# Attention on one core: the row maximum over 1024 keys as one reduction over two PSUM banks, with two score banks instead of four

## The reference

```
attn = einsum('bhcnd,bhcmd->bhcnm', q, k) * scale      # 1024 x 1024 for each head and chunk
attn = softmax(attn, axis=-1)                          # needs the maximum over the 1024 keys
o = einsum('bhcnm,bhcmd->bhcnd', attn, v)
out = o @ Wp.T + bp
```

## Time and profile before

| | us |
|---|---|
| median of 3 runs | 13767.46 (13765.76 to 13772.49) |
| the profiled execution, span | 13760.1 |
| outside the span, median less span | 7.4 |
| PE busy | 12819.6 (93%) |
| DVE busy | 9806.3 (71%) |
| ACT busy | 7890.2 (57%) |
| attention, first to last maximum reduction | 4550.0 to 12863.5 |

### The profile page before, as it was taken

One profiled execution on the slowest core, in us unless ns is written; L12 is line 12 of the kernel. 1 busy time (PEld: TensorE's weight loads), 2 busy tenths in 40 slices (PEclk: granted clock), 3 DMA queues, 4 the chain that ended last, 5 costly groups with the idle time before them and its releaser, 6 DMA issues. The chain is left out here.

```text
span 13760.1 us, 258672 instructions
## 1 busy us (share of the span) xinstructions
PE 12819.6 (93%) x76348; PEld 5285.8 (38%) x76348; DVE 9806.3 (71%) x18034; ACT 7890.2 (57%) x14774; POOL 2684.0 (20%) x2692
## 2 busy tenths in 40 slices
PE   6999999999993799999999999999999999999899
PEld 3545544544552233333333333333333333333233
DVE  7888888888886676777777777777777777677411
ACT  4666666666663365666665666666666666566511
POOL 3445444444441000000000000000000000000144
PEclk9999999999996799999999999999999999999999
DMA  2110110101104222222222232222222222222254
GB/s 73 21 21 15 21 20 16 21 15 21 21 15 134 67 61 67 65 62 63 67 65 63 61 71 63 60 68 66 61 62 66 67 63 61 66 63 64 62 127 105
DMA packets 853449, 773.62 MB, mean 56 GB/s; under 512 B 587076, under 2 KB 621348, under 8 KB 840740
## 3 DMA queue, kind: packets, MB, share of 16 engines
q1 hardware_dynamic: 850468, 747.29, 24.0%
q10 hardware_dynamic: 1536, 8.39, 0.3%
HBM read 510.50 MB, written 244.96 MB: 55 GB/s over the span
## 5 line engine op out<-in xcount | busy, mean ns | idle before, releaser
L1495 DVE TENSOR_REDUCE a_big<-a_mp 128x1 f32<-128x512 f32 x8192 | 5225.0, 685 | 2325.0 <-PE a_mp L1328 2060.3
L1414 ACT ACTIVATE a_ex<-a_sc 128x512 f32<-128x512 f32 x8192 | 4450.3, 599 | 2366.1 <-PE a_sc L1316 2121.6
L1328 PE MATMUL a_mp<-a_ks,a_qs 108*128 108x512 bf16 x8192 | 3188.5, 389 | 188.5 <-DVE a_big L1495 86.1
L1316 PE MATMUL a_sc<-a_qs,a_ks 111*128 111x512 bf16 x8192 | 3157.0, 387 | 125.3 <-issue 80.6
L849 DVE TENSOR_TENSOR r_prod<-r_pg,r_win 128x512 f32<-128x512 f32 x3584 | 2318.9, 683 | 533.1 <-PE r_pg L583 279.6
L1342 PE MATMUL a_po<-a_ex,a_va 128*32 128x512 f32 x16384 | 2221.0, 615 | 18.6 <-ACT a_ex L1414 17.8
L1230 POOL TENSOR_TENSOR a_pieces<-a_left,a_pieces 128x512 bf16<-128x512 f32 x256 | 295.4, 1154 | 7904.8 <-ACT a_pieces L1400 7904.8
L1316 PEld LDWEIGHTS a_sc<-a_qs,a_ks 111*128 111x128 bf16 x8192 | 797.2, 98 | 2529.3 <-ACT a_ex L1414 1807.7
L524 POOL TENSOR_TENSOR r_prod<-r_temp,r_win 128x512 f32<-128x512 f32 x1024 | 1214.8, 1207 | 1401.8 <-PE r_pl L632 621.3
L1328 PEld LDWEIGHTS a_mp<-a_ks,a_qs 108*128 108x128 bf16 x8192 | 802.3, 98 | 1598.8 <-DVE a_big L1495 1009.9
L587 PE MATMUL r_pg<-r_ident,r_spread 128*128 128x128 f32 x9216 | 1195.7, 278 | 112.0 <-DVE r_prod L849 93.3
(11 more groups left out here) (192 smaller groups left out, 11692.5 us busy)
## 6 DMA issues: line engine op xcount, KB each, us to landing
a_qs<-qk_parts SPq DMA_DIRECT2D x768, 144.0 KB
a_ks<-qk_parts SPq DMA_DIRECT2D x768, 144.0 KB
qk_parts<-a_pieces SPq DMA_DIRECT2D x128, 768.0 KB, 5.0
f_t<-mixed SPq DMA_DIRECT2D x48, 1536.0 KB, 16.4
a_tw<-second SPq DMA_DIRECT2D x512, 128.0 KB, 3.0
mixed<-a_t SPq DMA_DIRECT2D x256, 256.0 KB, 2.1
r_win<-first SPq DMA_DIRECT2D x128, 280.5 KB, 5.2
a_zw<-layered SPq DMA_DIRECT2D x192, 144.0 KB, 11.8
```

Of the source, the lines that this page charges most:

```text
L1316: pe.matmul(sc[x][:, :], ks[0:KROWS + NPART, p.h, head, 128 * kb:128 * kb + 128], qs[0:KROWS + NPART, p.h, head, CHUNK * qb:CHUNK * qb + C ...
L1328: pe.matmul(mp[half][:, :], qs[0:KROWS, p.h, head, 128 * q:128 * q + 128], ks[0:KROWS, p.h, head, CHUNK * half:CHUNK * half + CHUNK], star ...
L1414: nc.scalar.activation(ex[:, k % RING, :], sc[x][:, :], ACT.Exp, scale=scale).then_inc(exped.sem, 1)
L1495: nc.vector.tensor_reduce(big[:, x % 2, k // 2:k // 2 + 1], mp[x % 2][:, :], AX_X, ALU.max).then_inc(maxed.sem, 1)
```

## The change

The maximum banks become two pairs: `mp[0]` and `mp[1]` have 1024 columns each. The two halves of a row are written to the two halves of one pair, only the first of them waits (for the reduction two pairs back), and only the second signals. DVE makes one reduction of 1024 per row where it made two of 512, and the combination of the halves (L1503) goes. To have the banks for that, the score banks go from four to two: `score` waits for the exponential two before it. All eight PSUM banks are used before and after. Order on PE and ACT, tasks, DMAs and arithmetic are as before.

```diff
+SC_BANKS = 2
...
-    big = sb("big", [128, 2, HEADS * KB])
-    top = sb("top", [128, QUAD * KB])
+    big = sb("big", [128, HEADS * KB])
...
-    sc = [ctx.enter_context(nc.psum_tensor(f"a_sc{i}", [128, CHUNK], F32)) for i in range(QUAD)]
-    mp = [ctx.enter_context(nc.psum_tensor(f"a_mp{i}", [128, CHUNK], F32)) for i in range(2)]
+    sc = [ctx.enter_context(nc.psum_tensor(f"a_sc{i}", [128, CHUNK], F32)) for i in range(SC_BANKS)]
+    mp = [ctx.enter_context(nc.psum_tensor(f"a_mp{i}", [128, UNIT], F32)) for i in range(2)]
...
-            if not (isinstance(p.n, int) and p.n == 0 and k < QUAD):
-                pe.wait_ge(exped.sem, exped.at(p.n, k - QUAD + 1))
-            pe.matmul(sc[x][:, :], ks[0:KROWS + NPART, p.h, head, 128 * kb:128 * kb + 128],
+            if not (isinstance(p.n, int) and p.n == 0 and k < SC_BANKS):
+                pe.wait_ge(exped.sem, exped.at(p.n, k - SC_BANKS + 1))
+            pe.matmul(sc[x % SC_BANKS][:, :], ks[0:KROWS + NPART, p.h, head, 128 * kb:128 * kb + 128],
...
-            pe.wait_ge(maxed.sem, maxed.at(p.n, k - 1))
-            pe.matmul(mp[half][:, :], qs[0:KROWS, p.h, head, 128 * q:128 * q + 128],
-                      ks[0:KROWS, p.h, head, CHUNK * half:CHUNK * half + CHUNK],
-                      start=True, stop=True).then_inc(max_made.sem, 1)
+            if half == 0:
+                if k % (QUAD * KB) == 0:
+                    pe.wait_ge(stack_in[head // QUAD].sem, stack_in[head // QUAD].at(p.n, 16 * 12))
+                pe.wait_ge(maxed.sem, maxed.at(p.n, k - 1))
+            last = pe.matmul(mp[k % 2][:, CHUNK * half:CHUNK * half + CHUNK],
+                             qs[0:KROWS, p.h, head, 128 * q:128 * q + 128],
+                             ks[0:KROWS, p.h, head, CHUNK * half:CHUNK * half + CHUNK], start=True, stop=True)
+            if half == 1:
+                last.then_inc(max_made.sem, 1)
...
+            if x % 2 == 0:
+                return
+            k = 2 * t + x // 2
             dve.wait_ge(max_made.sem, max_made.at(p.n, k + 1))
-            nc.vector.tensor_reduce(big[:, x % 2, k // 2:k // 2 + 1], mp[x % 2][:, :],
-                                    AX_X, ALU.max).then_inc(maxed.sem, 1)
+            nc.vector.tensor_reduce(big[:, k:k + 1], mp[k % 2][:, :], AX_X, ALU.max).then_inc(maxed.sem, 1)
...
-            nc.vector.tensor_tensor(top[:, :], halves_of[0], halves_of[1], ALU.max).then_inc(m0.sem, 1)
```

More of the change, by code:

```diff
@@ L1062, in attention_phase @@
     v_done = Signal(sem("v_done"), 3)
-    max_made = Signal(sem("max_made"), 2 * HEADS * KB)
-    maxed = Signal(sem("maxed"), 2 * HEADS * KB, 2)
-    m0 = Signal(sem("m0"), 2)
+    max_made = Signal(sem("max_made"), HEADS * KB)
+    maxed = Signal(sem("maxed"), HEADS * KB, 2)
     m1 = Signal(sem("m1"), 2)
@@ L1320, in maximum @@
         def maximum(p, t, x):
-            k = 4 * t + x
-            head, q = divmod(k // 2, KB)
+            k = 2 * t + x // 2
+            head, q = divmod(k, KB)
             half = x % 2
-            if k % (2 * QUAD * KB) == 0:
-                pe.wait_ge(stack_in[head // QUAD].sem, stack_in[head // QUAD].at(p.n, 16 * 12))
-            pe.wait_ge(maxed.sem, maxed.at(p.n, k - 1))
-            pe.matmul(mp[half][:, :], qs[0:KROWS, p.h, head, 128 * q:128 * q + 128],
-                      ks[0:KROWS, p.h, head, CHUNK * half:CHUNK * half + CHUNK],
-                      start=True, stop=True).then_inc(max_made.sem, 1)
+            if half == 0:
[7 more added lines that the diff above has]
+                last.then_inc(max_made.sem, 1)
         def values(p, t):
@@ L1413, in exponentials @@
                     act.wait_ge(valued.sem, valued.at(p.n, t - 1))
-                nc.scalar.activation(ex[:, k % RING, :], sc[x][:, :], ACT.Exp, scale=scale).then_inc(exped.sem, 1)
+                nc.scalar.activation(ex[:, k % RING, :], sc[x % SC_BANKS][:, :], ACT.Exp, scale=scale).then_inc(exped.sem, 1)
         def outputs(p, g):
@@ L1492, in maximum @@
         def maximum(p, t, x):
-            k = 4 * t + x
+            if x % 2 == 0:
+                return
+            k = 2 * t + x // 2
             dve.wait_ge(max_made.sem, max_made.at(p.n, k + 1))
-            nc.vector.tensor_reduce(big[:, x % 2, k // 2:k // 2 + 1], mp[x % 2][:, :],
-                                    AX_X, ALU.max).then_inc(maxed.sem, 1)
+            nc.vector.tensor_reduce(big[:, k:k + 1], mp[k % 2][:, :], AX_X, ALU.max).then_inc(maxed.sem, 1)
         def negate(p, quad):
             n = p.n
-            halves_of = [big[:, half, 32 * quad:32 * quad + 32] for half in range(2)]
-            dve.wait_ge(maxed.sem, maxed.at(n, 64 * quad + 64))
-            nc.vector.tensor_tensor(top[:, :], halves_of[0], halves_of[1], ALU.max).then_inc(m0.sem, 1)
-            dve.wait_ge(m0.sem, m0.at(n, quad + 1))
+            top = big[:, 32 * quad:32 * quad + 32]
+            dve.wait_ge(maxed.sem, maxed.at(n, 32 * quad + 32))
             if not (isinstance(n, int) and n == 0 and quad == 0):
                 dve.wait_ge(neg_turned.sem, neg_turned.at(n, quad))
-            nc.vector.tensor_scalar(mparts[:, 0, :], top[:, :], -1.0, None, ALU.mult).then_inc(m1.sem, 1)
+            nc.vector.tensor_scalar(mparts[:, 0, :], top, -1.0, None, ALU.mult).then_inc(m1.sem, 1)
             dve.wait_ge(m1.sem, m1.at(n, quad + 1))
-            nc.vector.scalar_tensor_tensor(out=mleft[:, 0, :], in0=top[:, :], scalar=-1.0, in1=mparts[:, 0, :],
+            nc.vector.scalar_tensor_tensor(out=mleft[:, 0, :], in0=top, scalar=-1.0, in1=mparts[:, 0, :],
                                            op0=ALU.mult, op1=ALU.subtract).then_inc(m2.sem, 1)
```

## The result

| | before | after |
|---|---|---|
| median, range (5 runs each) | 13767.46 (13760.22 to 13772.49) | 13820.23 (13815.87 to 13835.89) |
| ratio to before, 95% interval | | 1.0038 (1.0025 to 1.0051) |
| the profiled execution, span | 13760.1 | 13816.1 |
| DVE busy | 9806.3 | 9521.8 |
| PE busy | 12819.6 | 12840.5 |

The change made the kernel slower, by some 53 us where I forecast none. It came out near the first rival's time (13831), inside the wide range (13700 to 13850) and outside the forecast's own (13738 to 13792).

What follows compares the result with a forecast made beforehand. Waits, not a full engine, bound the kernel: PE and DVE in a ring in plain steps. 13760.1 - 21 (units) + 20 (loop heads) - 10 + 8 (ends) = 13757, predicted 13765 us, no change; own range 13738 to 13792, wide 13700 to 13850.

Steps and rivals of the forecast that it cites:

- first rival: Slower: DVE's late task work at twelve places a unit costs 0.22 each, not 0.133; 13831 us, chance 0.33.
- What bounds the kernel: In attention, waits decide: PE and DVE wait for each other in plain steps (9 of 32); PE bounds task steps.
- ring of maxima: Plain steps: maximum matmuls wait for DVE's reductions of full banks and DVE waits for PE, setting V to V' at 3.31.
- Part 1: DVE's 1024-column reduction lasts 1.21 us, the next starting 1.13 after; 0.14 us less per step, worth nothing by itself.
- Parts 2 and 3: Plain steps: no maximum matmul waits, ACT's exponentials then bind; 3.31 falls to 3.10, turn and back to 3.28; gain 1.94 us a unit.
- Part 4: Task bank handed over later: DVE's work starts 0.33 later, costing 1.60 us a unit; bounds 0 and 0.30 each.
- twelve places: Turn to back, four a unit, 0.15 each; eight other task steps, 0.12 to 0.13 each; 756 in all.
- my own signs of being wrong: Plain steps staying at 3.31, wide reduction over 1.3, or task steps growing by less than 0.05 or over 0.2.
- Part 5: 29 loop heads, where PE restarts at half clock and s2 waits for ACT: +0.7 each (0.3 to 1.5), +20 us.
- Part 6: The ends: first unit's maximum rows faster, -10 us; last unit's steps 2.56 to 2.87, 27 steps, +8 us.
- Slower: the hand-over costs more: Rival: PE stands still for DVE's late task work at 756 places, 0.22 each instead of 0.133; 13831 us, chance 0.33.
- The score banks never bind: Rival: PE runs a plain step in 2.84, another 139 us less, 13626; against it, e3's exponential ends late; chance 0.04.

Runs made afterwards that it cites:

- e2: Kernel before with two score banks and four single maximum banks, each read by its own 512-column reduction; 13648.67 us, ratio 0.9913.
- e3: Kernel before with three score and three maximum banks in rotation, reductions of 512, task work where it was; 13459.21 us, ratio 0.9774.
- e1: Changed kernel with DVE doing the task work of the step before ahead of a step's reductions; 13643.58 us, ratio to before 0.9911.
- e7: The changed kernel measured once more, unaltered, as reference for other runs; 13834.45 us, ratio to the kernel before 1.0044.
- e4: Kernel before with two score banks for four and their waits, its two single maximum banks kept; 13791.88 us, ratio 1.0020.
- e6: Kernel before with only DVE's order changed, task work of the step before ahead of the four reductions; 13855.65 us, ratio 1.0064.
- e8: Kernel before with task work first and a turn's broadcast copy reading PSUM, not SBUF, leaving out output normalization; 13824.18 us, ratio 1.0043.

## Why the prediction was wrong

**What bounds the kernel: right.** The ring of maxima set the plain steps: with it loosened they fall from 3.31 to 3.10 (e2) and to 2.84 (e3).

**Part 1, the wide reduction: right.** 1.22 measured for 1.21, the next starting 1.14 after for 1.13; worth nothing by itself (e1 against e2).

**Parts 2 and 3: right.** Plain steps 3.10, bound by ACT, s1' at V + 2.56. Turn steps 3.28. The gain of 1.94 us a unit was there: e1 has it whole. Small errors: at 24 the step went from 3.31 to 3.37, at 0 in the middle of a round from 3.51 to 3.37.

**Part 4, the hand-over: the step that failed, by its size.** The twelve places were right and the mechanism was right. The price was put at 1.60 us a unit and measured 2.79: 1.19 x 63 = 75 us, more than the whole miss of 55. By kind: turn to back 0.25 for 0.15, four times (0.40), the eight others 1.75 together for 1.00 (0.75), and 0.04 at two places that I had at nothing. By term, all of them short on the same side:
- The reduction starts at V + 0.11, not 0.07, and the task work 1.14 behind it for 1.13: V + 1.25 for 1.20. Twelve times 0.05 is 0.60.
- The signal. Where the load carries the wait itself, it follows the end of DVE's work by 0.05 to 0.06 (qk: 8095.42 behind 8094.68 + 0.68), as estimated. At six places, the four back tasks and the two out tasks behind a back, PE has two waits, and the trace has a wait instruction of 0.05 ahead of the load; there it follows by 0.11 to 0.12 (turn: 8025.57 behind 8025.46) for 0.05: six times 0.06 is 0.36.
- The rest, 0.23, is mostly the weight load that waits, 0.10 (2.68 for 2.58) for 0.07 at five qk and out places (0.15), and the two places that I had at nothing (0.04). What is left isn't resolved further.

My outer bound of 0.30 a place had all this in it, but the range was made with 0.22 at most, and 0.23 was measured. That the time still lies in it is in part luck: the phases ahead of the attention were 9 us shorter in the profiled execution, and the first unit won 4 more than I gave it. What was wrong was the value taken, 0.13: no term in it had an allowance for being short, and every one was. One of my own signs of being wrong came up, too: task steps were not to grow by over 0.2, and a qk step grew by 0.21, turn to back by 0.22 (3.53 for 3.31).

**Part 5, the heads: right, as far as it can be told.** +0.76 each, give or take 0.4, for +0.7: 22 us for 20. The other kernels with two score banks, less what their hand-overs cost, give 0.8 (e7), 0.6 (e2), 0.5 (e4) and 0.4 (e1). V' came at A + 4.3 for 4.6, and the next V at A + 8.1 on average, as worked out. But the 7.21 of before was one head: the average is 7.6, and 12.6 us was the longest absence of ACT (7.7 to 12.6). That the total fits is in part luck.

**Part 6: right in sign and about in size.** The first unit is 15 us shorter (from the first maximum matmul to the first score 94.6 for 109.1), for 10. A step of the last unit is 2.88 for 2.87.

The two traces add up. From step 4 of the first unit to step 4 of the last, after is 75.2 us longer: some 0.9 (1.79 / 2) in each unit of the loop and 0.76 at each head, but at most 0.4 in the three units outside the loop, which I had counted in full. The rest of the last unit adds 7.4. Against that, the phases ahead of the attention are 8.8 shorter, the stretch up to the first score 14.5, the first steps 2.0 and what follows the attention 1.4: +56, by which the spans differ. No instruction of the phases outside the attention was changed, so the 8.8 and 1.4 are differences between executions.

**The rivals.** "Slower: the hand-over costs more" is what happened, with 0.23 a place for its 0.22, and 13831 against 13820 and 13834 measured (after, e7). "The score banks never bind" was excluded for the reason given: plain steps stayed at 3.10, with s1' waiting for e3. The Trainium skill's rule that stood against the change ("Perfetto Trace Analysis", Optimizing Scalar/DVE Operations) points the right way: on an engine that is idle a third of the time, grouping made what followed late, and undoing it (e2) took 172 us off. e1 narrows it: with the urgent work in front of the group, the same grouping costs nothing.

## What to carry to other kernels

Before two operations are made one, look at what stands behind them on the same engine and at its slack: the first of two small ones can run while the second's input is still being made, a wide one can't, and here 0.38 us of lateness at twelve places outweighed what the plain steps won. Moving the urgent work ahead is not good by itself: with four maximum banks in pairs it won 1.3% (e1), with two single ones it lost 0.6% (e6). When work is only just late by your sum, charge each place with the exposed weight load and the signal in full. When two rings of banks bind in turn, try equal shares before you widen one at the cost of the other. Against four score and two maximum banks, two score banks and two pairs lost 0.4%, two and four single ones won 0.9%, and three and three won 2.3%.

## What the runs showed of the hardware

A DVE copy between two SBUF tiles (128x512 fp32) can stand still while POOL works: 0.43 us alone, 1.40 when POOL's subtraction had started 0.05 before it (e6), 1.03 when it had started 0.41 before in e1, where it was hidden; both end 0.28 after POOL does. With its input in PSUM it takes 0.69 and is never held (690 to 692 ns over 256 copies in e8). The Trainium skill ("SBUF — State Buffer", Who interferes with whom) has the rule: DVE and GpSimd share a pair of ports, a copy can be of the kind that wants it, whichever issues first keeps it for its whole instruction, and a DVE operation with at most one SBUF input outside those modes doesn't contend. The runs agree for a copy that starts behind POOL's operation; no run here has one that starts ahead of it.

One reduction over two PSUM banks costs no more than its columns: 1.22 us for 1024, against 0.68 for 512, so 0.54 for the second bank.

A task of PE that has to wait loses more than the wait: up to 0.10 us for the weight load that is no longer hidden (2.68 for 2.58 at a qk task), and some 0.06 more where a wait instruction of its own stands before the load (0.11 to 0.12 behind the end of DVE's work, for 0.05 to 0.06).
